# Linear attention on one Trainium2 core: its quadratic part over blocks of 64 tokens instead of 128

## The reference

```python
q, k = sigmoid(x @ Wq + bq), sigmoid(x @ Wk + bk);  v = x @ Wv + bv      # per head
normal = arange(L) + 1
sink_in = normal / dot(q + EPS, cumsum(k) + EPS)
src_out = normal / dot(k + EPS, cumsum(q) + EPS)
cons_sink = dot(q + EPS, cumsum(k * src_out) + EPS) / normal
cons_src = clip(dot(k + EPS, cumsum(q * sink_in) + EPS) / normal, -1, 1)
sink_alloc, cons_src = sigmoid(cons_sink), exp(cons_src)
src_comp = cons_src / cumsum(cons_src) * normal
qs, vs = q * sink_in / normal, v * src_comp
kv = cumsum(einsum('bhld,bhlm->bhldm', k, vs))       # state of 16 x 16 a head, after each token
out = einsum('bhld,bhldm->bhlm', qs, kv) * sink_alloc
h = layernorm(x + out @ Wo + bo);  h = layernorm(h + gelu(h @ W1 + b1) @ W2 + b2)
x = layernorm(x + h)
# then: each token goes to the expert of its largest logit: x = layernorm(x + relu(x @ fc)**2 @ pj.T)
```

## Time and profile before

| what | before |
|---|---|
| median of 3 runs | 819.48 us (818.86 to 822.41) |
| profiled execution | 819.06 us |
| its span | 817.3 us |
| TensorE (PE) busy | 784.7 us, 96% |
| DVE busy | 572.2 us, 70% |
| ACT busy | 317.6 us, 39% |
| POOL busy | 338.4 us, 41% |
| mean granted TensorE clock | 0.991 |

### The profile page before, as it was taken

The page is one execution under the profiler, slowest core; times in us unless marked ns, Lnnn a source line. Parts: engine busy times, 40 slices in busy tenths (PEclk is TensorE's granted clock), DMA queues, the critical chain, the costliest instruction groups (busy, mean ns, idle before and its releaser), DMA issues.

```text
span 817.3 us, 18774 instructions
## 1 busy us (share of the span) xinstructions
PE 784.7 (96%) x6848; PEld 602.6 (74%) x6848; DVE 572.2 (70%) x1209; ACT 317.6 (39%) x586; POOL 338.4 (41%) x548
## 2 busy tenths in 40 slices
PE   8999999999999999999999989999999999999994
PEld 4476787687687677777777777788997778777762
DVE  7978768889899899899899894764663333433432
ACT  2332424433543543543444433343213444333442
POOL 8300402423434535525425444675334433334434
PEclk9989999999999999999999999999999999999998
DMA  8799997101000100100000101894569998888850
GB/s 279 231 331 325 321 313 237 52 1 48 6 15 16 51 8 21 53 8 21 28 7 9 41 7 32 303 360 159 188 195 398 373 343 323 308 315 296 292 194 13
DMA packets 75193, 133.22 MB, mean 163 GB/s; under 512 B 5725, under 2 KB 54111, under 8 KB 75104
## 3 DMA queue, kind: packets, MB, share of 16 engines
q1 hardware_dynamic: 71648, 123.05, 45.0%
q0 software_dynamic: 3168, 8.46, 2.8%
...
## 4 chain that ended last, share of the span: by engine, by line
PE 84%; DVE 6%; POOL 5%; issue 3%; ACT 1%; DMA 1%; POOLq 0%; ACTq 0%; DVEq 0%
PE bank L1000 11%; PE bank L965 10%; PE bank L852 7%; PE bank L884 6%; PE bank L895 6%; PE bank L864 5%; PE bank L656 5%; PE bank L814 4%; PE bank L776 4%; PE bank L1012 4%; PE bank L980 4%; PE bank L830 3%; PE bank L665 3%; PE bank L686 2%; PE bank L694 1%
## 5 line engine op out<-in xcount | busy, mean ns | idle before, releaser
L1321 POOL TENSOR_SCALAR vare<-mv 128x1 f32<-128x1 f32 x96 | 24.4, 254 | 255.7 <-DVE mv L1595 252.7
L965 PE MATMUL bank<-xsT,fc 128*128 128x128 f32 x800 | 94.4, 276 | 0.5 <-issue 0.5
L965 PEld LDWEIGHTS bank<-xsT,fc 128*128 128x128 f32 x800 | 91.4, 192 | 3.6 <-issue 3.4
L1588 DVE TENSOR_TENSOR sm<-bank,upto 128x512 f32<-128x512 f32 x128 | 79.3, 681 | 16.6 <-PE bank L776 16.5
L1000 PE MATMUL bank<-pj,act 128*128 x336 | 76.1, 379 | 0.8 <-DVE act L1783 0.8
L1180 ACT ACTIVATE relu<-bank 128x512 f32<-128x512 f32 x68 | 40.2, 595 | 91.4 <-PE bank L965 63.2
L852 PE MATMUL bank<-n1T,w1s 128*128 128x256 f32 x256 | 68.9, 392 | 2.6 <-ACT n1T L1124 1.8
L884 PE MATMUL bank<-n1T,w1s 128*128 128x256 f32 x256 | 69.3, 394 | 1.7 <-ACT n1T L1140 0.9
L1000 PEld LDWEIGHTS bank<-pj,act 128*128 128x128 f32 x336 | 62.2, 190 | 8.7 <-issue 1.1
L895 PE MATMUL bank<-w2s,hT 128*128 128x256 f32 x256 | 66.9, 385 | 0.0
L864 PE MATMUL bank<-w2s,hT 128*128 128x256 f32 x256 | 64.5, 380 | 0.0
...
## 6 DMA issues: line engine op xcount, KB each, us to landing
...
```

What stands on the lines that cost most here:

```text
L965: last = nc.tensor.matmul(h_bank[n][:, chunk(f)], fc[:, at, k, chunk(4 * n + f)], xsT[:, k, :], start=(k == 0), stop=(k == KT - 1))
L1588: nc.vector.tensor_tensor(sm[:, n], BANK4[n][:].rearrange("p (h t) -> p h t", h=4), upto[:].unsqueeze(1).broadcast_to([P, 4, P]), ALU.mult ...
```

## The change

Scores are made over 64 tokens in place of 128. A chunk of 128 tokens is two parts of `Q = 64`, each with scores of its own, and two chunks are worked on together as a block (`ND = 2` blocks a group). All four chunks' keys are transposed and copied first; then one step `p_upd` makes the contributions of all eight parts to the state, on tiles of 64 rows by 32 columns, into `ps0` and `pa`; DVE takes them to `sums`, masked by the head's parity, and adds them up in a chain, which gives the state at the beginning of each 64 tokens; the last goes to `carried` for the next group. `p_pairs` (twice a group) uses tiles of 32 rows by 64 columns, `p_mix` (twice) makes the state's part on 32 by 32 tiles and the values on 64 by 32 tiles, the part's number choosing the bank (`pm`, `ps1`); ACT copies both. `p_mask` has 8 steps in place of 16. `p_out` makes both chunks' outputs in the two halves of `pa`. The mask `same_head` is gone. All lists of the order are new; two are shown.

```diff
+ND, Q = NC // 2, P // 2
...
 PE_ORDER = [
...
+    ("b_turn", 0), ("p_share2", 0), ("d_count", 0), ("b_turn", 1), ("a_proj", 0), ("a_proj", 1), ("a_proj", 2),
+    ("a_proj", 3), ("b_up", 0), ("p_kt", 0), ("a_proj", 4), ("b_up", 1), ("p_kt", 1), ("a_proj", 5), ("b_down", 0),
+    ("p_kt", 2), ("b_down", 1), ("p_kt", 3), ("b_up", 2), ("p_upd", 0), ("b_up", 3), ("p_pairs", 0), ("b_down", 2),
+    ("b_down", 3), ("p_mix", 0), ("a_dots1", 0), ("b_up", 4), ("p_out", 0), ("b_up", 5), ("b_down", 4), ("b_up", 6),
+    ("b_down", 5), ("b_up", 7), ("b_down", 6), ("h_turn", 0), ("a_share1", 0), ("c_route", 0), ("h_turn", 1),
+    ("b_down", 7), ("h_up", 0), ("p_pairs", 2), ("h_up", 1), ("c_route", 1), ("h_down", 0), ("h_up", 2),
+    ("h_down", 1), ("h_up", 3), ("h_down", 2), ("h_up", 4), ("h_down", 3), ("p_mix", 2), ("a_dots2", 0),
+    ("h_up", 5), ("c_route", 2), ("p_out", 2), ("c_route", 3), ("h_down", 4), ("h_up", 6), ("a_comp", 0),
+    ("c_logit", 0), ("h_down", 5), ("c_back", 0), ("h_up", 7), ("h_down", 6), ("h_down", 7),
...
 DVE_ORDER = [
...
+    ("p_share2", 0), ("a_proj", 0), ("d_count", 0), ("a_proj", 1), ("c_sum2", 0), ("a_proj", 2), ("a_proj", 3),
+    ("a_proj", 4), ("a_proj", 5), ("c_sum2", 1), ("a_prod", 0), ("p_state", 0), ("p_mask", 0), ("p_mask", 1),
+    ("p_mask", 2), ("p_mask", 3), ("c_sum3", 0), ("c_sum2", 2), ("c_sum3", 1), ("b_half", 0), ("c_sum3", 2),
+    ("p_sums", 0), ("p_sums", 1), ("c_sum2", 3), ("a_dots1", 0), ("a_share1", 0), ("c_sum3", 3), ("p_mask", 4),
+    ("p_mask", 5), ("p_mask", 6), ("p_mask", 7), ("a_scan2", 0), ("a_scan2", 1), ("a_dots2", 0), ("b_add", 0),
+    ("p_sums", 2), ("p_sums", 3), ("a_comp", 0), ("c_choose", 0),
...
-        summed, state = s1("summed", [P, KT, 2 * DH]), s1("state", [P, KT, P])
-        same_head = s1("same_head", [P, P])
+        sums, carried = s1("sums", [P, 2, NC, KT * 2 * DH]), s1("carried", [P, KT * 2 * DH])
...
+        def sums_of(k):
+
+            return sums[:, k % 2, k // 2]
+
+        def state_at(k):
+
+            return sums_of(k - 1) if k else carried[:]
+
+        def ktok_of(c):
+
+            return ktok[:, c] if c < 2 else xat[:, c - 2].rearrange("p m t -> p (m t)")
...
-            def pairs(g, half, c):
-
-                if c == 0:
-                    ev["kp"].wait(pe, g, 2)
+            def pairs(g, half, i):
+                d = i // 2
+                if d == 0:
                     for par in range(2):
                         ev[f"qm{par}"].wait(pe, g, KT)
-                    ev["sig"].wait_if_any(pe, g + 1, 4)
-                    ev["v"].wait_if_any(pe, g + 1, 4)
-                elif c == 1:
+                    ev["summed"].wait(pe, g, 2)
+                else:
                     ev["rden"].wait_if_any(pe, g + 1, 1)
-                elif c == 2:
                     ev["scaled"].wait_if_any(pe, g + 1, 4)
-                else:
-                    ev["cons"].wait_if_any(pe, g + 1, 1)
-                ev["summed"].wait(pe, g, c)
-                ev["r1"].wait(pe, g, c)
-                ev["sm"].wait(pe, g, 4 * c)
-                for m in range(KT):
-                    for i in range(4):
-                        rows = slice(32 * i, 32 * i + 32)
-                        last = nc.tensor.matmul(BANK4[i][:, m * 2 * P:(m + 1) * 2 * P], kT[rows, half, m, chunk(c)],
-                                                qm[rows, :, m, chunk(c)], start=True, stop=True,
-                                                skip_group_check=True)
-                        if m == KT - 1:
-                            last.then_inc(S["s"], 1)
+                ev["r1"].wait(pe, g, 2 * d)
+                ev["sm"].wait(pe, g, 4 * d)
+                for c in range(2):
+                    for m in range(KT):
+                        at = (2 * c + m) * P
+                        for part in range(2):
+                            keys = slice(Q * part, Q * part + Q)
+                            tokens = slice((2 * d + c) * P + Q * part, (2 * d + c) * P + Q * part + Q)
+                            for j in range(4):
+                                rows = slice(32 * j, 32 * j + 32)
+                                last = nc.tensor.matmul(BANK4[j][keys, at:at + P], kT[rows, half, m, tokens],
+                                                        qm[rows, :, m, tokens], start=True, stop=True,
+                                                        skip_group_check=True)
+                                if (c, m, part) == (1, KT - 1, 1):
+                                    last.then_inc(S["s"], 1)
...
                 else:
-                    ev["xrtc"].wait_if_any(pe, g - 2, c)
+                    ev["ktc"].wait(pe, g, c)
...
-            def mix(g, half, c):
-
-                fresh = half == 0 and c == 0
-                if g == 0 and c == 0:
+            def update(g, half, _):
+
+                ev["ktc"].wait(pe, g, NC)
+                ev["v"].wait(pe, g, 4)
+                ev["qp"].wait(pe, g, KT)
+                ev["kp"].wait(pe, g, KT)
+                ev["sig"].wait_if_any(pe, g + 1, 4)
+                ev["v"].wait_if_any(pe, g + 1, 4)
+                for c in range(NC):
+                    for m in range(KT):
+                        for j in range(HPT // 2):
+                            at = m * P + 32 * j
+                            to = c * KT * 32 + 32 * m
+                            for part, dst in enumerate((ps0, pa)):
+                                keys = slice(Q * part, Q * part + Q)
+                                last = nc.tensor.matmul(dst[32 * j:32 * j + 32, to:to + 32],
+                                                        ktok_of(c)[keys, at:at + 32], diag(half, c)[keys, 4 * m + j],
+                                                        start=True, stop=True, skip_group_check=True)
+                last.then_inc(S["upd"], 1)
+
+            def mix(g, half, i):
+                d = i // 2
+                if g == 0 and d == 0:
                     pe.wait_ge(tables_in, 16 * 8)
-                ev["ktc"].wait(pe, g, c + 1)
-                if not fresh:
-                    ev["st"].wait(pe, g, c)
-                    apart(pe)
+                if d:
+                    ev["xrtc"].wait_if_any(pe, g - 2, 2)
+                ev["st"].wait(pe, g, (3, 2 * NC - 1)[d])
+                ev["sm"].wait(pe, g, 4 * d + 2)
+                begun = set()
+                for c in range(2):
+                    for part, dst in enumerate((pm, ps1)):
+                        k = 2 * (2 * d + c) + part
+                        if half == 0 and k == 0:
+                            continue
+                        for m in range(KT):
+                            at = (2 * c + m) * Q
+                            for j in range(HPT // 2):
+                                rows = slice(32 * j, 32 * j + 32)
+                                nc.tensor.matmul(dst[rows, at:at + Q], state_at(k)[rows, 32 * m:32 * m + 32],
+                                                 qs[rows, m, Q * k:Q * k + Q], start=(part, j) not in begun, stop=False,
+                                                 skip_group_check=True)
+                                begun.add((part, j))
+                ev["v"].wait(pe, g, 4)
+                for c in range(2):
                     for m in range(KT):
-                        nc.tensor.matmul(pm[:, chunk(m)], state[:, m, :], qs[:, m, chunk(c)], start=(m == 0), stop=False,
-                                         skip_group_check=True)
-                ev["v"].wait(pe, g, 4)
-                for m in range(KT):
-                    for j in range(HPT // 2):
-                        if m == 0:
-                            ev["sm"].wait(pe, g, 4 * c + j + 1)
+                        at = (2 * c + m) * Q
                         for e in range(2):
-                            last = nc.tensor.matmul(
-                                pm[32 * j:32 * j + 32, chunk(m)], vpad[:, half, c, 4 * m + j, 32 * e:32 * e + 32],
-                                sm[:, j, 2 * m + e, :],
-                                start=(fresh and m == 0 and e == 0), stop=False, skip_group_check=True)
+                            for j in range(HPT // 2):
+                                if c == m == e == 0:
+                                    ev["sm"].wait(pe, g, 4 * d + j + 1)
+                                for part, dst in enumerate((pm, ps1)):
+                                    keys = slice(Q * part, Q * part + Q)
+                                    last = nc.tensor.matmul(
+                                        dst[32 * j:32 * j + 32, at:at + Q],
+                                        vpad[keys, half, 2 * d + c, 4 * m + j, 32 * e:32 * e + 32],
+                                        sm[keys, j, 4 * c + 2 * m + e, :], start=False, stop=False,
+                                        skip_group_check=True)
                 last.then_inc(S["av"], 1)
-                for m in range(KT):
```

(61 more changed lines are left out.)

206 lines of the change are left out of this document (96 added, 110 removed), and 7 rows, old and new, of tables (DVE_LAST, POOL_LAST).

## The result

The changed kernel takes 857.8 us (851.5 to 863.0, 4 runs) beside 820.8 us of the kernel before on the same chip: a ratio of 1.0448, 95% interval 1.035 to 1.0546. It is slower by 37 us where 28 us less was forecast. Of its four runs two lie near 852 us, the profiled one among them, and two near 863 us, so a difference of a few us to its median tells little.

The account below looks back on a forecast made before the run. TensorE's queue was taken to bound the kernel: 21.3 us from six groups, 6 us from groups 0 and 7 and 1 us at the start make 28.3 us off 819.48 us, so 791 us (783 to 799; with rivals 781 to 816).

Parts of the forecast that it names:

- the rival of 826 us: State products run one after another, 3.46 us a block instead of 0.87 us, giving 826 us; chance 0.08.
- I take 0.054 us: Time assumed for a turn of 64 columns on the array, by columns alone, with no extra per turn.
- The update: The contributions to the state, 128 instructions once a group on eight tiles: taken as 0.70 us.
- from 11.0 to 6.75: TensorE's time per group for pairs, mix and update, in us, before and after: 4.25 us less a group.
- The rival of slow turns: Narrow turns cost 0.087 us instead of 0.054 us, as the update's do, giving 807 us; chance 0.10.
- I take 0.7 us of new idle a group, between 0 and 1.5 us: TensorE's added waiting per group for the carry chain, leaving 3.55 us net gain in each of six groups.
- the sign of being wrong: The forecast is wrong if TensorE's idle time per group passes 3 us.
- The clock as a surcharge: A half-clock stretch after a stall loses some 1.7 us; one such stall more lies inside the range.
- The masked copies: Two copies out of PSUM on DVE, between update and pairs: little delay counted, as feed-forward steps stand around each.
- 3 us each: Gain counted for group 0 and for group 7, which are nearer to being bound by latency.
- DVE's fall: DVE's time per group falls by 5.2 us, to about 52.3 us, with TensorE at 58.6 us the longer queue.
- The start: Without POOL's head mask the third group's inputs load sooner, cutting TensorE's 1.66 us wait: 1 us comes off.

Follow-up runs that it names:

- e1: The kernel before with 576 products that nobody reads (1152 MATMULs) put behind its last one: 838.06 us, one run.
- e7: The kernel before with pair products cut into four and value products into two, of 64 columns each, neighbours on different row strips: 846.2 us, ratio 1.0319.
- e8: The changed kernel with the update's 64 products issued twice in a row in each group: 890.6 us, ratio 1.0857.
- e10: e5 with update, pairs and mix as whole steps, each two feed-forward steps apart, and other orders to match: 830.2 us, ratio 1.0123.
- e5: The changed kernel with DVE's choice of experts moved behind the scaled queries and TensorE's count behind the third projection: 844.6 us, ratio 1.0288.
- e11: e10 with own orders for second and eighth periods, first group's shifts in one piece, a feed-forward step before the first transpose: 845.2 us, ratio 1.0302.
- e12: e10 with only the second period's own order and the choice at the end of the seventh period: 832.0 us, ratio 1.0155.

## Why the prediction was wrong

**The sizes of the steps.** The pairs were right (1.21 and 1.13 us a block with the seams for 1.08), state products do run side by side (0.80 us for 48, where one after another they would take 2.6 us, so the rival of 826 us is out), and eight tiles work at once. The values were mis-sized: 1.41 us a block for 0.905. "I take 0.054 us" a turn rested on the earlier trace rows, where four tiles share a turn; with eight, a MATMUL is due every 6.75 ns (0.054 us by eight), and PE runs one in 11 ns (e1). The update took 1.21 us for 0.70. Over five steady periods pairs, mix and update together fell from 10.8 to 8.4 us a group, not from 11.0 to 6.75, each counted to the start of the step behind it, waits left out.

The Trainium skill (TensorEngine Tiling (Array Packing), Gotcha 1: PSUM Pressure) says that different row tiles can't access one PSUM bank at the same time. Where the strips write different partitions of a bank the 0.80 us for 48 don't agree with it.

**The rival of slow turns** had the right price (0.087 us against 0.088 measured for the values) by luck: it took the update's turn on four tiles for a cost of few columns. On four tiles 64 columns took 0.0575 us a turn (e7). What the densest short products show instead is a time per MATMUL near 10 ns, whatever their columns: 11 ns with 64 columns on eight tiles and 10 ns with 32 columns on four (e1, from start to start), 9.5 ns with 32 columns on eight (the update). Its size, 13 us over eight groups (8.4 us for 6.75), is near the 16 us by which the rival stood beside the forecast. It alone would have led to some 804 us, not 858.

**What had no place in the sum: the supply of instructions.** The step that failed is "I take 0.7 us of new idle a group, between 0 and 1.5 us". It holds a term for the chain and none for the arrival of instructions, which was put at nothing without a reason: the counts stood in the same working (64, 64 and 128 instructions a block, 128 a group for the update), the packets stood on the page, and no rate of them was asked for. The runs showed 4.8 us of new idle a steady period (5.5 instead of 0.7), past the 3 us that the prediction itself named as the sign of being wrong; of the 5.5 us 2.5 are issue and 1.8 wait for the choice, told below. At 256 instructions in 3.46 us, a run of short products costs 13.5 ns an instruction, so 27 ns a MATMUL with its weight load, more than twice the 10 ns in which PE runs one that is there (e1). That makes 29 us of idle over the whole kernel: e1 shows the mechanism, the landings of the packets show it in the changed kernel, e8 makes more of it by more instructions in the same place, and e10 less of it by spacing the same ones. What this idle alone is worth in time no run shows, since the clock and the chain moved with it.

**The clock as a surcharge.** "One such stall more" became nine stretches at half the clock, 47.8 us without the one that ends the span, for two, 10.2 us, in the kernel before. One of them, behind a stall within the values (length, PE, weight loads, DVE, ACT, POOL, granted clock):

```profile
82.52:86.16 3.64, 0.00 (x0) 0.00 (x0) 3.57 (x5) 0.00 (x0) 0.00 (x0) 1.00 1.09 326
86.90:90.30 3.40, 3.40 (x35) 2.69 (x26) 1.56 (x3) 0.47 (x1) 0.00 (x0) 0.51 1.09 333
```

PE did nothing for 3.64 us; the 3.4 us from 86.90 us on are granted 0.51, the lower level. Taken at half of each stretch, an estimate that counts idle time too, 23.9 us were lost, 18.8 more than before. Of the 47.8 us 37.5 lie in the first group and the eighth period, which lost 10.4 and 5.4 us; the stops for instructions stand in the same places (8.1 and 3.4 us), and no run tells the two apart.

**The chain.** 0.7 us of new idle a group was taken for `a_comp` to `p_share2`. There it was more than enough: L699 waits 1.9 us in all. The masked copies, counted as little, cost PE little: 0.9 us, once. But the same shortening of PE's work at the period's end exposed the step behind it on DVE: the choice, and with it the count and the scaled queries, 7 to 13 us by e5. The prediction looked at who waits for the chain and not at what is queued behind it on DVE, though it asked that question of the masked copies.

**Groups without projections.** 3 us each were to be gained in the first and last group; they lost. Four transposes, an update, copies, pairs, masks and values in a row have to be covered by something, and in the second and eighth period the projections that cover them elsewhere are missing. e10 still loses 14.4 us there, and gains 1.3 us in the steady periods. Stops that end behind a packet's landing make 13.2 us in these stretches of e10 (5.0, 4.6 and 3.6), none in the kernel before; e10's eighth period also waits 3.7 us for the choice. How much of the 14.4 us each cause is worth is open: e11 and e12 moved these waits without a gain.

**Put together**, in us of span against the forecast of 28.3 less: in five steady periods 11.9 from PE's own work (1.9 gained for 4.25 a period), 20.7 from idle time (4.8 more for 0.7), and some 29 in the start, the first group and the second and eighth period, together the 62 by which it was off. DVE's fall was right (51.5 us in a steady period, forecast 52.3) and worth nothing, since PE's queue stayed the longer one. The start came out as forecast in its cause: PE's wait for the third group's inputs fell from 1.7 to 0.8 us (L682), but the first group behind it lost more.
